# Layer 1 attention, other orders inside a pass: each score block right ahead of a value block on TensorE, the second behind the output projection

## The reference

```python
qkv = jnp.einsum('bsd,od->bso', x, w_qkv)          # 32 query heads of 64, 8 key/value heads
q, k, v = jnp.split(qkv, [q_size, q_size + kv_size], axis=-1)
q = _rms_norm(q, q_norm_w)
k = _rms_norm(k, k_norm_w)
q, k = _rope(q, k, PAST_LENGTH)
scores = jnp.einsum('bhqd,bhkd->bhqk', q, k_rep) * scale
scores = scores + _sliding_mask(s, s, PAST_LENGTH)  # a query sees itself and the 63 keys before it
probs = jax.nn.softmax(scores, axis=-1)
attn = jnp.einsum('bhqk,bhkd->bhqd', probs, v_rep)
attn = attn.transpose(0, 2, 1, 3).reshape(b, s, q_size)
return jnp.einsum('bso,do->bsd', attn, w_out)
```

## Time and profile before

| | us |
|---|---|
| median of 3 runs | 530.66 (529.77 to 531.55) |
| the profiled execution: its own time | 531.71 |
| its span in the trace | 529.9 |
| PE busy | 476.8 (90% of the span) |
| DVE busy | 387.5 (73%) |
| ACT busy | 337.3 (64%) |
| POOL busy | 233.0 (44%) |

### The profile page before, as it was taken

The page is one execution under the profiler, slowest core; times in us unless marked ns, Lnnn a source line. Parts: engine busy times, 40 slices in busy tenths (PEclk is TensorE's granted clock), DMA queues, the critical chain, the costliest instruction groups (busy, mean ns, idle before and its releaser), DMA issues.

```text
span 529.9 us, 10779 instructions
## 1 busy us (share of the span) xinstructions
PE 476.8 (90%) x3848; PEld 399.9 (75%) x3848; DVE 387.5 (73%) x675; ACT 337.3 (64%) x940; POOL 233.0 (44%) x167
## 2 busy tenths in 40 slices
PE   2899997999999966999999999989997797999994
PEld 2454654788889956888889998878985686788884
DVE  4455598778562789998889898889899875543634
ACT  3555556634643439988888898859887698332230
POOL 0377537221640745665556556355638523500001
PEclk9999998999999997999999999989999899999999
DMA  8400010032410000000000000001000222000101
GB/s 274 167 18 2 2 41 0 1 119 90 117 51 13 1 1 1 22 21 13 10 22 21 21 22 21 21 1 41 22 30 32 61 61 82 1 0 1 41 0 40
DMA packets 8611, 19.96 MB, mean 38 GB/s; under 512 B 1392, under 2 KB 2928, under 8 KB 8432
## 3 DMA queue, kind: packets, MB, share of 16 engines
q1 hardware_dynamic: 8560, 19.29, 11.7%
HBM read 18.23 MB, written 1.05 MB: 36 GB/s over the span
## 4 chain that ended last, share of the span: by engine, by line
PE 72%; DVE 10%; ACT 8%; issue 4%; POOL 3%; DMA 1%; DVEq 0%; POOLq 0%; ACTq 0%; SPq 0%
PE psum L383 16%; PE psum L385 15%; PE psum L384 15%; PE psum L614 4%; PE psum L602 4%; PE psum L430 4%; PE psum L592 4%; ACT probs L846 4%; PE psum L448 4%; PE psum L573 2%; POOL rms_inverse L1249 1%; PE psum L582 1%; DVE minus_max L1122 1%; DMA raw_chunks<-in_w 1%; PE psum L565 1%
## 5 line engine op out<-in xcount | busy, mean ns | idle before, releaser
L846 ACT ACTIVATE probs<-psum,minus_max 128x128 f32<-128x128 f32 x256 | 92.0, 390 | 17.9 <-PE psum L592 10.8
L1240 POOL TENSOR_TENSOR rope_sin_part<-qkv_rows,sin_weighted 128x640 f32<-128x640 f32 x32 | 48.9, 1549 | 50.5 <-DVE rope_cos_part L1091 27.6
L1249 POOL TENSOR_TENSOR rms_inverse<-rms_inverse,minus_half 128x20 f32<-128x20 f32 x16 | 63.1, 3945 | 1.3
L818 ACT CAST hidden_high<-hidden 128x512 fp32r<-128x512 f32 x32 | 19.9, 620 | 62.5 <-DVE hidden L1037 62.5
L846 ACT ACTIVATION_READ_ACCUMULATOR probs<-psum,minus_max 128x1 f32 x256 | 58.2, 227 | 0.0
L1122 DVE TENSOR_REDUCE minus_max<-psum 128x4 f32<-128x512 f32 x64 | 41.2, 685 | 18.3 <-PE psum L592 18.3
L383 PE MATMUL psum<-x_t_high,ug_high 128*128 128x512 f32 x128 | 51.2, 400 | 0.0
L1116 DVE TENSOR_TENSOR probs<-probs,prob_inverse 128x512 f32<-128x512 f32 x64 | 49.3, 770 | 2.2
L385 PE MATMUL psum<-x_t_high,ug_low 128*128 128x512 f32 x128 | 50.7, 396 | 0.0
L384 PE MATMUL psum<-x_t_low,ug_high 128*128 128x512 f32 x128 | 50.4, 394 | 0.0
L383 PE MATMUL psum<-qkv_high,x_t_high 128*128 128x384 f32 x128 | 47.3, 369 | 0.0
(11 more groups left out here) (146 smaller groups left out, 1378.7 us busy)
## 6 DMA issues: line engine op xcount, KB each, us to landing
raw_chunks<-in_ug SPq DMA_DIRECT2D x8, 512.0 KB, 3.9
raw_chunks<-in_wout SPq DMA_DIRECT2D x16, 256.0 KB, 2.8
raw_chunks<-in_qkv SPq DMA_DIRECT2D x8, 384.0 KB, 3.3
raw_chunks<-in_x SPq DMA_DIRECT2D x2, 512.0 KB, 4.5
raw_chunks<-in_w SPq DMA_DIRECT2D x2, 512.0 KB, 6.3
down_tree<-in_down SPq DMA_DIRECT2D x1, 1024.0 KB, 8.3
x_rows<-in_x_rows SPq DMA_DIRECT2D x2, 512.0 KB, 4.8
raw_chunks<-in_down SPq DMA_DIRECT2D x2, 512.0 KB, 4.0
```

Of the source, the lines that this page charges most:

```text
L846: e = nc.scalar.activation(pr[:, c, q, :], o[:, q * P:(q + 1) * P], ACT.Exp, bias=negm[:, c, q:q + 1], accum_out=psum1[:, c, q:q + 1])
L1240: last = nc.gpsimd.tensor_tensor(ov[:, :, :, z, :], rv[:, :, :, 1 - z, :], sv[:, :, :, z, :], ALU.mult)
L1249: nc.gpsimd.tensor_tensor(r, r, half[:], ALU.pow).then_inc(rr_done, 1)
```

## The change

The tables of the four engines get another order; nothing else differs, and every step, shape and instruction is the same. On PE the second score block moves from ahead of `turn_p(5,3)` and `out1(6,1)` to behind them, and so right ahead of the second value block, which stays where it was; the first value block moves up past a projection part to stand right behind the first score block; and `proj1` 0 goes ahead of two transposes in place of between them. ACT and DVE follow with their own moves, and POOL takes `rms_inverses` one item further at the end of the pass in place of the beginning of the next, which changes its order only against what stands between passes.

```diff
-    ("proj1", 1, 0), ("turn_p", 5, 1), ("scores1", 4, 0), ("proj1", 1, 2), ("pv1", 5, 0), ("proj1", 1, 3), ("scores1",
-    4, 1), ("turn_p", 5, 3), ("out1", 6, 1), ("pv1", 5, 1), ("turn1q", 3, 1)]
+    ("turn_p", 5, 1), ("turn_p", 5, 2), ("scores1", 4, 0), ("pv1", 5, 0), ("proj1", 1, 2), ("proj1", 1, 3), ("turn_p",
+    5, 3), ("out1", 6, 1), ("scores1", 4, 1), ("pv1", 5, 1), ("turn1q", 3, 1)]
...
-GPSIMD_PASS = [("rms_inverses", 3), ("sines", 2), ("wout", 5)]
+GPSIMD_PASS = [("sines", 2), ("wout", 5), ("rms_inverses", 2)]
```

More of the change, by code:

```diff
@@ L43 @@
 NIT = B * KV
-TENSOR_PASS = [("turn1q", 4, 0), ("turn1k", 4), ("out1", 6, 0), ("proj1", 1, 1), ("turn_p", 5, 0), ("turn_p", 5, 2),
-    ("proj1", 1, 0), ("turn_p", 5, 1), ("scores1", 4, 0), ("proj1", 1, 2), ("pv1", 5, 0), ("proj1", 1, 3), ("scores1",
-    4, 1), ("turn_p", 5, 3), ("out1", 6, 1), ("pv1", 5, 1), ("turn1q", 3, 1)]
[L49 to L54, removed]
-GPSIMD_PASS = [("rms_inverses", 3), ("sines", 2), ("wout", 5)]
+TENSOR_PASS = [("turn1q", 4, 0), ("turn1k", 4), ("out1", 6, 0), ("proj1", 1, 1), ("turn_p", 5, 0), ("proj1", 1, 0),
+    ("turn_p", 5, 1), ("turn_p", 5, 2), ("scores1", 4, 0), ("pv1", 5, 0), ("proj1", 1, 2), ("proj1", 1, 3), ("turn_p",
+    5, 3), ("out1", 6, 1), ("scores1", 4, 1), ("pv1", 5, 1), ("turn1q", 3, 1)]
+SCALAR_PASS = [("squares", 2), ("turn1q", 4, 1), ("proj1", 1, 1), ("turn1k", 4), ("turn1q", 4, 0), ("turn_p", 5, 0),
+    ("turn_p", 5, 1), ("turn_p", 5, 2), ("proj1", 1, 0), ("exps", 4, 0), ("pv1", 5, 0), ("exps", 4, 1), ("proj1", 1,
+    2), ("wout", 5), ("proj1", 1, 3), ("turn_p", 5, 3), ("exps", 4, 2), ("pv1", 5, 1), ("exps", 4, 3)]
+VECTOR_PASS = [("probs", 5, 3), ("values1", 2), ("rope_sums", 3), ("maxima", 4, 0), ("maxima", 4, 1), ("square_sums",
+    2), ("normed", 3), ("maxima", 4, 2), ("pv1", 5, 0), ("maxima", 4, 3), ("probs", 4, 1), ("probs", 4, 0),
+    ("cosines", 2), ("probs", 4, 2), ("pv1", 5, 1)]
+GPSIMD_PASS = [("sines", 2), ("wout", 5), ("rms_inverses", 2)]
 PASSES = NIT + max(step[1] for step in TENSOR_PASS + SCALAR_PASS + VECTOR_PASS + GPSIMD_PASS)
```

## The result

The change made the kernel slower, and by about what was forecast: 543.44 us (542.77 to 544.21, 3 runs) against 530.66, a ratio of 1.0234 [1.0208, 1.026]. Forecast were 544.4. The profiled execution took 544.21 us with a span of 542.2, against 531.71 and 529.9 before; PE's share of the span fell from 90 to 88%.

The account below looks back on a forecast made before the run. PE was taken to bound the full passes; 10.6 (eight regular) + 0.45 + 3.6 + 1.0 = 15.7, less 2 in late passes, gave 13.7 more, 544.4 us on the median of 530.66; range 537 to 551.

Parts of the forecast that it names:

- PE bounds the full passes, so each wait counts in full: Passes 5 to 16: PE is busy 30.00 of 30 us, so anything added to its list or any wait counts fully.
- The wait, 1.53: PE's second value block waits for the first one's bank, returned by DVE behind the second score block's first maxima: 1.53 us.
- Shape changes, -0.2 a pass: On PE in full passes, fewer changes between full-array products and products on 64 rows or columns: -0.2 us a pass.
- the direct pair: On PE, a score block directly into a value block: this change of shape was taken to cost 0.11 us.
- Full pass +1.33: A full pass goes from 15.35 us, less 0.2 for shapes, plus 1.53 of wait, to 16.7: +1.33.
- No second wait, by 0.15 us: At `proj1` 0, DVE's second read-out returns the bank at 6.6 us, PE wants it at 6.75: fits by 0.15.
- R2: Rival: a second wait binds, the chain over DVE setting the pass at 17.0 to 17.3; 548 to 551 us, chance 17%.
- Behind passes 13 and 16, +1.8 each: The new wait is swallowed there, but another engine's chain starts later with the second score block: +1.8 us each.
- Pass 5 and pass 14: Pass 5: new wait runs alongside one of 0.89 for ACT, +0.45; behind pass 14: longer pass partly covers 0.72, +1.0.
- R3: Rival: TensorE's clock falls with each new wait, up to 1.6 us each, +19 more, 563 us; chance 4%.
- Late passes, -2: Passes 17 to 21: DVE's third division starts ahead of POOL's `ug_low`; bounds 0 and -4, taken as -2 us.
- R1: Rival: faster, the bank wait doesn't decide and only shape changes count; 526 us, chance 5%.

Follow-up runs that it names:

- e3_pe_alone: The kernel before with only PE's new order, the other engines keeping their old tables; 551.92 us, ratio 1.0399 to before.
- e11_and_q_copy: The changed kernel with both value-block read-outs moved forward on DVE and ACT's copy of q moved up; 529.54 us, ratio 0.9968 to before.
- e7_first_pair_alone: The kernel before with only the first value block moved up on PE, directly behind the first score block; 529.37 us, ratio 0.9976 to before.
- e1_readout_first: The changed kernel with DVE's read-out of the first value block ahead of both maxima of the second score block; 534.54 us, ratio 1.0082 to before.
- e9_second_readout_alone: The changed kernel with only DVE's read-out of the second value block moved ahead of the third division; 544.14 us in a single run.
- e12_pool_alone_timed: The kernel before with only POOL's new order, timed; 530.2 us, ratio 0.9992 to before.
- e6_pool_alone: The kernel before with only POOL's new order, in a single run; 529.3 us.

## Why the prediction was right, point by point

- *PE bounds the full passes, so each wait counts in full.* Shown: 1.45 of wait less 0.35 for the shape changes is 1.10 a pass, 1.07 was measured, and a full pass without waits takes 15.00.
- *The wait, 1.53.* Shown, by the timeline and by `e3_pe_alone`, where one more maxima in front makes it 0.60 longer. It measured 1.45: the start of PE behind DVE's end is 0.05 and not 0.14. The row at 411.54 that gave 0.14 has transposes behind the read-out, in a late pass.
- *Shape changes, -0.2 a pass.* The sign was right, the size half of it: `e11_and_q_copy` has -0.35. The mis-sized term is the direct pair, taken at 0.11 from a late pass. In a full pass the 16 products of a score block take 278.52 - 277.53 = 0.99 ahead of a value block, against 0.98 ahead of a projection: going from score block to value block costs no more than going on to a full-array product. With 0 for it the prediction's sum would have been -0.3. `e7_first_pair_alone` bears it out (-0.19 for the first pair, forecast -0.08). The Trainium skill's rule on mode switches, which the prediction quotes (TensorEngine Tiling (Array Packing), Key Properties), says that each direct pair still switches; what the runs show is that this switch costs no more than the one that it replaces, so the prediction's "the trace agrees, 0.11 for the direct pair" was a misreading. The same trace would have shown it: in the late pass the extra 0.11 lies at the start of the score block, whose weight load had waited for ACT's copy of k, and not at its end: the first two products show 0.33 in place of 0.22, and the other fourteen add 0.83 in both. The weight load and the first two products there, and then the first two products in the full pass of the change:

```profile
432.45 0.97 PEld L592 LDWEIGHTS psum<-k_t,q_t 64*128 64x128 f32 x16 [0.28 <-ACT k_t L834]
432.45 0.33 PE L592 MATMUL psum<-k_t,q_t 64*128 64x64 f32 x2
```

```profile
277.53 0.22 PE L592 MATMUL psum<-k_t,q_t 64*128 64x64 f32 x2
```

- *Full pass +1.33:* measured +1.07, by these two terms (0.08 and 0.15), which both erred the same way.
- *No second wait, by 0.15 us.* Right for the change, with a margin of 0.2. But the margin was made by the first wait, which the prediction left unsaid, and `e1_readout_first` shows it: take the first away and the second appears. R2 was a true mechanism in the wrong kernel.
- *Behind passes 13 and 16, +1.8 each.* The mechanism held in both: the end of the layer norm's wait stands 357.70 - 349.40 = 8.30 behind the second score block, before 346.80 - 338.40 = 8.40; the first score block of pass 17 stands 9.50 behind the second of pass 16, before 9.59. The sum was right behind 16 (+1.58) and not behind 13 (+0.16), where a fall of the clock went missing. Where it did not go missing, in `e9_second_readout_alone`, the row is +1.74.
- *Pass 5 and pass 14:* +0.45 and +1.0 forecast, +2.37 and +2.54 measured. "Both waits run at the same time" held in pass 5: the wait of 0.89 for ACT is gone, one of 1.36 stands in its place, and a new one of 0.57 for ACT stands ahead of the second score block. Up to the start of that value block +0.76 had come together; the other 1.61 came behind it, with the fall of the clock. In pass 14 the wait of 1.50 for ACT takes back what the clock had given behind pass 13, the new wait follows, and the clock falls behind it. Over both passes +2.8 was forecast and +2.70 measured, but `e9_second_readout_alone`, without that last fall, has +1.83: the forecast was about 1 too high there, and the fall made it good. The term left out is the clock's.
- *R3, at 4%, was true in two of twelve waits.* The one in pass 5 cost 1.6 us, the one in pass 14 0.9. That the total came so near has luck in it: eight full passes were taken 2.1 us too dear together, pass 5 1.9 too cheap, and the rest of the sum 1.2 too dear.
- *Late passes, -2.* Measured -2.1, by two large terms: -3.80 and +1.72. The held division was the right place for the first; that the gain would be partly given back one pass later was not seen. That POOL's order would move `ug_low` onto the next division did not happen by itself (`e12_pool_alone_timed`); the number -2 was a choice between bounds.
- *R1* would have needed DVE to read out before the second score block. `e1_readout_first` does just that and still is 4 us slower than before, so even R1's 526 was out of reach with these tables.

## What to carry to other kernels

Where results go round a ring of banks, moving one result on the matrix engine changes who has to have read out by then: for each moved claim find the result that has its bank, then its reader, then what stands ahead of that read-out on the reader's list. Price a new wait with what it hides as well; behind the first there stood a second and a third here, each within 0.7 us, and only with all three gone did the new order show its gain of 0.35 us a pass. Take the price of a transition from a stage that is bound by that engine, and see where in the step the extra time lies: a late operand had passed for a change of shape here. And read neighbouring intervals together, over several executions: time won in one was twice given back in the next.

## What the runs showed of the hardware

- The idle time in brackets is less than what a wait costs: at `proj1` 0 it reads 0.48 and the step starts 0.72 late, at the value block 1.37 and 1.45. The shown duration of the last product before a wait reaches into the wait: 286.38 - 1.37 is the shown end of the score block, 285.0, while the next step would have started at 284.93. Starts are the measure.
- The length of a wait didn't decide whether TensorE's clock fell from 2.4 to 1.2 GHz. In the changed kernel it fell behind waits of 1.36 (twice) and 2.41 us, and stayed up behind the other ten new waits (1.37 and 1.38) and behind one of 3.08. Nor did a second wait shortly before decide it: the two of 1.36 had one, of 0.57 and 1.50 us, ahead of the score block, but in `e3_pe_alone` waits of 0.57 and 1.95 stand in the same place and the 16 products behind show 1.09, as at the upper level. The same kernel even does both. `e6_pool_alone` and `e12_pool_alone_timed` are one kernel, and behind the same wait for the layer norm the clock stayed up in the first and fell in the second:

```profile
346.32 0.38 PE L383 MATMUL psum<-wout_high,out_t_high 128*128 128x256 f32 x1 [2.62 <-DVE x_rows L962]
```

```profile
346.32:349.72 3.40, 3.40 (x27) 1.00 0.00 0
```

```profile
346.60 0.58 PE L383 MATMUL psum<-wout_high,out_t_high 128*128 128x256 f32 x1 [2.63 <-DVE x_rows L962]
```

```profile
346.60:350.00 3.40, 3.40 (x16) 0.56 0.00 0
```

- What a fall costs depends on what comes next. In full passes, which TensorE bounds, it cost 1.6 us (after, pass 5; `e3_pe_alone`, pass 15: 406.63 - 397.67 = 8.96 against 7.34). Behind the layer norm it cost nothing over two passes: the interval there is 18.23 in `e6_pool_alone` and 19.55 in `e12_pool_alone_timed`, the next one 19.08 and 17.75, together 37.31 and 37.30, because PE, where it comes sooner, waits 1.26 for ACT ahead of the next score block.
